# First attention of a decoder layer: row maxima taken by pairs of half-array products, values two steps behind

## What is computed

```python
q = (x @ Wq + bq).reshape(b, s, NH, HD).transpose(0, 2, 1, 3)
k = (x @ Wk + bk).reshape(b, s, NH, HD).transpose(0, 2, 1, 3)
v = (x @ Wv + bv).reshape(b, s, NH, HD).transpose(0, 2, 1, 3)
scores = jnp.einsum('bhqd,bhkd->bhqk', q, k) / jnp.sqrt(HD)
mod = jax.nn.sigmoid(x @ cg_W + cg_b + (cons_vec @ am_W + am_b))
scores = scores * mod.transpose(0, 2, 1)[..., None]
probs = jax.nn.softmax(scores, axis=-1)
ctx = jnp.einsum('bhqk,bhkd->bhqd', probs, v)
```

## Time and profile before

| | |
|---|---|
| median of 3 runs | 4114.03 us (4112.56 to 4117.21) |
| the profiled execution: time, span in the profile | 4116.67 us, 4114.9 us |
| granted TensorE clock, mean over the span | 0.905 of full speed |
| `attend_narrow`, first maximum to last copy | about 216 to 1074.5 us |
| its first score | 256.8 us |

### The profile page before, as it was taken

How to read it: one execution, slowest core, us unless ns; L and a number is a source line. 1 busy time by engine, 2 the same in 40 slices (tenths; PEclk the granted TensorE clock), 3 DMA queues, 4 the chain that set the end, 5 groups by cost and what they waited for, 6 DMA issues and landing times. The chain is left out here.

```text
span 4114.9 us, 58511 instructions
## 1 busy us (share of the span) xinstructions
PE 3605.2 (88%) x17196; PEld 2369.5 (58%) x17196; DVE 2374.9 (58%) x4296; ACT 1487.1 (36%) x2363; POOL 1038.5 (25%) x798
## 2 busy tenths in 40 slices
PE   8889999999799968799966587855899999999999
PEld 6644444545244426444445344434788888888888
DVE  5577777777266645566546588866433333333345
ACT  3236666666434333243433233321222222222222
POOL 4510000000033334333333400001333333333332
PEclk9979999999799988799987667767999999999999
DMA  7854444442333326533333665622000000000001
GB/s 248 275 66 63 63 63 63 63 63 37 80 83 82 82 72 216 151 83 82 85 114 128 136 84 81 90 76 74 16 15 15 0 15 15 15 0 15 0 5 36
DMA packets 218079, 303.68 MB, mean 74 GB/s; under 512 B 27679, under 2 KB 133511, under 8 KB 217927
## 3 DMA queue, kind: packets, MB, share of 16 engines
q1 hardware_dynamic: 213703, 297.65, 32.5%
q10 hardware_dynamic: 4224, 4.19, 0.3%
HBM read 182.23 MB, written 119.54 MB: 73 GB/s over the span
## 5 line engine op out<-in xcount | busy, mean ns | idle before, releaser
L564 DVE TENSOR_REDUCE an_m<-an_psm 128x1 f32<-128x1024 f32 x512 | 605.0, 1220 | 194.9 <-PE an_psm L488 193.3
L544 ACT ACTIVATE an_probs<-an_pst 128x512 f32<-128x512 f32 x1024 | 533.5, 603 | 258.4 <-PE an_pst L515 257.9
L2349 POOL TENSOR_TENSOR ex_hb<-ex_hid,ex_ha 128x512 fp32r<-128x512 f32 x288 | 375.7, 1305 | 773.8 <-DVE ex_ha L2430 773.8
L2400 ACT ACTIVATE ex_gated<-ex_pg 128x512 f32<-128x512 f32 x288 | 172.4, 598 | 926.1 <-PE ex_pg L47 926.1
L2428 DVE TENSOR_TENSOR ex_hid<-ex_gated,ex_pu 128x512 f32<-128x512 f32 x288 | 198.2, 688 | 480.6 <-PE ex_pu L47 478.1
L488 PE MATMUL an_psm<-an_ks,an_qs 95*128 95x512 f32 x1024 | 368.8, 444 | 33.4 <-DMA an_vs<-scr_v 29.8
L515 PE MATMUL an_pst<-an_qs,an_ks 96*128 96x512 f32 x1024 | 340.2, 411 | 10.8 <-issue 6.3
L488 PEld LDWEIGHTS an_psm<-an_ks,an_qs 95*128 95x128 f32 x1024 | 181.3, 199 | 270.8 <-issue 206.9
L2383 PE MATMUL ex_py<-ew_a,ex_hb 128*128 128x256 f32 x1152 | 321.7, 279 | 0.0
L2383 PE MATMUL ex_py<-ew_b,ex_ha 128*128 128x256 f32 x1152 | 321.6, 279 | 0.0
L2383 PE MATMUL ex_py<-ew_a,ex_ha 128*128 128x256 f32 x1152 | 321.4, 279 | 0.0
(11 more groups left out here) (358 smaller groups left out, 7057.9 us busy)
## 6 DMA issues: line engine op xcount, KB each, us to landing
an_qs<-scr_q SPq DMA_DIRECT2D x64, 256.0 KB, 11.6
an_ks<-scr_k SPq DMA_DIRECT2D x64, 256.0 KB, 13.5
ac_qs<-scr_xq SPq DMA_DIRECT2D x64, 256.0 KB, 7.7
ca_qs<-scr_cq SPq DMA_DIRECT2D x24, 512.0 KB, 8.3
ca_ks<-scr_ck SPq DMA_DIRECT2D x24, 512.0 KB, 10.0
mc_qs<-scr_mq SPq DMA_DIRECT2D x24, 512.0 KB, 8.7
mc_ks<-scr_mk SPq DMA_DIRECT2D x24, 512.0 KB, 10.3
scr_q<-in_ab SPq DMA_DIRECT2D x16, 512.0 KB, 2.8
```

The source lines that it names most:

```text
L544: act.activation(probs[:, s % 2, j], pst[:, (GH * s + j) % RING], ACT.Exp, scale=HD ** -0.5).then_inc(exp_done, 1)
L564: dve.tensor_reduce(m1[:, hq, col:col + 1], psm[:, n % 2], AX.XY, ALU.max).then_inc(mx_done, 1)
L2349: pool.tensor_tensor(hb[:, f], hid[:, f % 2], ha[:, f].bitcast(F32), ALU.subtract).then_inc(b_done, 1)
L2400: act.activation(gated[:, f % 2], pg[:, f % 2], ACT.Silu).then_inc(gated_done, 1)
```

## The change

It is in `attend_narrow` alone, but for ten semaphores of the row transfers, which `decoder_layer` now makes and passes in (`moved`).

- **Layout.** The low-by-low combination is dropped (three combinations, 48 rows). `qs` holds the 48 rows twice, at rows 0 to 47 and 64 to 111, with a row of maxima behind each copy. `ks` holds keys 0 to 511 in the upper half of the array's rows and keys 512 to 1023 in the lower half; where one half holds keys, the other holds zeros.
- **Maxima in pairs.** The two products of a unit now contract over 48 rows each, one in rows 0 to 47, one from row 64, into the two banks of `psm`.
- **Scores.** Still one product per head and step, now over all 128 rows, the other half's zero keys included.
- **Values two steps behind** (`LAG = 2`), with `probs` four steps deep, across the borders of groups too; after a score with j = 1, or at the end of the step for a first key block.
- **Units** run 14 steps ahead (`LEAD`), so the last four units of a group fall into its own first two steps.
- **The rows of maxima** go through POOL's queue: per row four writes, a wait, two reads (one per copy), a wait. SP keeps loads (13 a group instead of 9) and stores.
- **Smaller:** DVE negates inside the reduction (L569 goes) and no longer copies `pacc`; ACT copies both halves. POOL and DVE fill more blocks before the first group.

```diff
-        qs, ks = k.sb("qs", [LAST, NG, GH, S], FR), k.sb("ks", [LAST, NG, GH, S], FR)
+        qs, ks = k.sb("qs", [P, NG, GH, S], FR), k.sb("ks", [P, NG, GH, HALVES, S // HALVES], FR)
...
-        probs = k.sb("probs", [P, 2, GH, CH])
+        probs = k.sb("probs", [P, TURNS, GH, CH])
...
+                for r, (qp, kp) in enumerate(((0, 0), (0, 1), (1, 0))):
+                    if first and r == 2:
+
+                        sp.wait_ge(filled, QFILLS + FILLS * slot)
+                        sp.wait_ge(filled_first, KFILLS)
+                    for h in range(HALVES):
+                        at = slice(h * HROW + r * HD, h * HROW + (r + 1) * HD)
+                        sp.dma_start(qs[at, slot].bitcast(F32),
...
-                last = pe.matmul(psm[:, n % 2, kh], qs[0:MROW, slot, j, q0:q0 + P], ks[0:MROW, slot, j, kh * CH:(kh + 1) * CH],
-                                 start=True, stop=True)
-                if kh == 1:
-                    last.then_inc(mx_ready, 1)
+                for h in range(HALVES):
+                    at = slice(h * HROW, h * HROW + DATA)
+                    last = pe.matmul(psm[:, n % 2, h], qs[at, slot, j, q0:q0 + P], ks[at, slot, j, h], start=True, stop=True)
+                last.then_inc(mx_ready, 1)
+
+            def scores(G, slot, s, j):
+                qh, kc = divmod(s, KC)
+                h, c = divmod(kc, KC // HALVES)
+                n = GH * s + j
+
+                pe.wait_ge(exp_done, EXP0 + NST * G + last_use(n) + 1)
+                pe.matmul(pst[:, bank[n]], ks[:, slot, j, h, c * P:(c + 1) * P],
+                          qs[:, slot, j, qh * CH:(qh + 1) * CH], start=True, stop=True).then_inc(st_ready, 1)
...
+            def step(b, g, s, before, more):
...
+                ahead, n0 = units_of(s)
+                late = before is not None and before[2] % KC == 0
+                for j in range(GH):
+                    scores(G, g, s, j)
+                    if j == 1 and before is not None and not late:
+                        values(*before)
+                    if j % 2 == 0:
+                        if ahead == 0:
+                            unit(G, g, b, n0 + j // 2)
+                        elif more:
+                            unit(G + 1, (g + 1) % NG, b + (g + 1) // NG, n0 + j // 2)
+                if late:
+                    values(*before)
...
+                pool.wait_ge(m_ready, CPB * G + hq + 1)
+                pool.sem_inc(row_seen, 1)
                 turned = scr["m"][hq].rearrange("(c b r) -> b c r", b=4, r=32)
                 for q in range(4):
-                    sp.dma_start(turned[q], mrows[32 * q:32 * q + GH * NT, hq].bitcast(F32)).then_inc(m_out[hq], 16)
+                    pool.dma_start(turned[q], mrows[32 * q:32 * q + GH * NT, hq].bitcast(F32)).then_inc(m_out[hq], 16)
+                pool.wait_ge(m_out[hq], 64 * G + 64)
+                pool.sem_inc(row_seen, 1)
+                for h in range(HALVES):
+                    row = h * HROW + DATA
+                    pool.dma_start(qs[row:row + 1, slot, :, hq * CH:(hq + 1) * CH].bitcast(F32),
+                                   scr["m"][hq:hq + 1].rearrange("o (j n) -> o j n", j=GH)).then_inc(mrow_in[slot][hq], 16)
+
+                pool.wait_ge(mrow_in[slot][hq], 32 * uses + 32)
...
-                    dve.tensor_reduce(m1[:, hq, col:col + 1], psm[:, n % 2], AX.XY, ALU.max).then_inc(mx_done, 1)
+                dve.tensor_reduce(mneg[:, hq, col:col + 1], psm[:, n % 2], AX.XY, ALU.max, negate=True).then_inc(mx_done, 1)
...
-                dve.tensor_copy(ev[:, 1], pacc[:]).then_inc(acc_dve, 1)
```

More of the change, by code:

```diff
@@ L434, in store, with group @@
             def store(G, qh):
[L435 to L438, removed]
+                sp.wait_ge(acc_out, CPB * G + qh + 2)
                 sp.dma_start(scr["craw"][bass.ds(G * P, P), qh * CH:(qh + 1) * CH], ev[:, qh]).then_inc(ev_out[qh], 16)
-            def group(b, g, ahead):
+            def group(b, g, more, first):
                 G = b * NG + g
[L443 to L450, removed]
+                if more:
+                    load(G + 2, (g + 2) % NG, first)
+                for qh in range(CPB):
+                    store(G, qh)
@@ L452, in _ @@
             for qh in range(CPB):
                 sp.sem_inc(ev_out[qh], 16)
[L454 to L458, removed]
+            load(0, 0, True)
+            load(1, 1, True)
+            for g in range(NG):
+                group(0, g, True, g < 2)
+            with sp.Fori(1, B - 1) as b:
                 for g in range(NG):
-                    group(b, g, 2)
+                    group(b, g, True, False)
@@ new lines, in step, with rest, border @@
+                if late:
+                    values(*before)
+            def rest(b, g, more):
+                G = b * NG + g
+                for s in range(LAG, NSTEP):
+                    step(b, g, s, (G, g, s - LAG), more)
+            def border(b, g, more):
+                for s in range(LAG):
+                    step(b + (g + 1) // NG, (g + 1) % NG, s, (b * NG + g, g, NSTEP - LAG + s), more)
+            pe.sem_inc(pv_done, PV0)
+            pe.wait_ge(filled_first, KFILLS)
+            for n in range(PER * LEAD):
+                unit(0, 0, 0, n)
@@ L528, in _ @@
+            for s in range(LAG):
+                step(0, 0, s, None, True)
             with pe.Fori(0, B - 1) as b:
                 for g in range(NG):
-                    group(b, g, True)
+                    rest(b, g, True)
+                    border(b, g, True)
             for g in range(NG):
-                group(B - 1, g, g < NG - 1)
+                rest(B - 1, g, g < NG - 1)
+                if g < NG - 1:
+                    border(B - 1, g, g + 1 < NG - 1)
+            for s in range(NSTEP - LAG, NSTEP):
+                values(B * NG - 1, NG - 1, s)
@@ L534, in _ @@
         @block.scalar
         def _(act):
[L536 to L549, removed]
@@ new lines, in _ @@
+            act.sem_inc(exp_done, EXP0)
+            act.sem_inc(acc_out, 1)
+            for s in range(LAG):
+                step(0, s)
+            with act.Fori(0, B - 1) as b:
+                for g in range(NG):
+                    G = b * NG + g
+                    rest(G)
+                    border(G)
+                    copy_out(G, 1)
+            for g in range(NG):
+                G = (B - 1) * NG + g
+                rest(G)
+                if g < NG - 1:
+                    border(G)
+                copy_out(G, 1)
```

207 lines of the change are left out of this document (114 added, 93 removed).

## The result

The changed kernel takes 4281.59 us (median of 4 runs, 4278.49 to 4297.44) against 4115.62 for the kernel before (4 runs, 4112.56 to 4119.7): a ratio of 1.0419, interval 1.0402 to 1.0436. It is slower, as forecast, but by 166 us where 48 were predicted; the range ended at 4190. The profiled execution of after took 4279.64 us against 4116.67 before, +163.

The account below looks back on a forecast made before the run. PE was taken to bound the step. Units +75, values' wait -5, group borders -14, last group -5 and start -3 gave +48 on 4116.67, 4165; less 2.6 to the median, 4162 us. Range 3965 to 4190.

Parts of the forecast that it names:

- The step: PE, middle of a group: six changes of tile shape make a unit 0.86 us instead of 0.705, +75 us in all.
- Rivals 1 to 4: Steps: 1 free changes (0.24); 2 only way back costs (0.08); 3 second load uncovered (0.09); 4 halves serial, changes free (0.03).
- Groups: Units +75 us, values no longer waiting for ACT -5, group borders -14.
- The border's gain: Group borders: values spread over the next steps remove 0.94 us, 15 times, -14 us.
- Last group: Steps without maxima, values two steps behind: PE alone sets 2.14 us instead of 2.60, -5 us.
- Start: First score after 28 units instead of 32, with more loads: -3 us, 0 if the row is late by 3.
- The row of maxima: Row transfers on POOL's queue: 4.4 to 18 us each, with 18 to 20 us available, so nothing added.
- rival 5: A row of maxima over 20 us on POOL stalls PE by the excess; 5 us over would be 155; chance 0.02.
- the likeliest case: Every change of tile shape costs and weight loads overlap: 4140 to 4190 us, chance 0.50.

Follow-up runs that it names:

- the loads behind the row: Changed kernel, but SP issues the loads of the group after next only once the group's second row of maxima has landed: 4188.54 us, ratio 1.0172.
- maxima of 64 rows: Kernel before, with maxima contracting over the 64 rows that hold data instead of 95, no pairs: 4356.53 us, ratio 1.0456.
- scores in a half: Changed kernel with loads after the second row of maxima, and scores contracting over the 49 rows that hold their keys: 4087.36 us, ratio 0.9927.
- both units together: Changed kernel with loads after the second row of maxima, and both units of a step issued behind its first score: 4103.38 us, ratio 0.997.
- with the whole array: All of the change but its layout (96 rows, unpaired full-array products), with loads after the second row of maxima: 4114.0 us, ratio 0.9993.

## Why the prediction was wrong in size

Its time is the sum of terms, so each is held against its own measurement. The run with the loads behind the row isolates the row; it took 4184.70 us in its profiled execution, +68 on before, and after took another +95.

- **The step: right.** Forecast 3.39 us, measured 3.37; score to score across a unit 0.86 forecast, 0.86 measured; every change of tile shape pays, the two halves overlap. Rivals 1 to 4 asked for steps of 2.6, 2.97, 3.6 or a pair 0.235 apart, and none is there. The price of 0.195 a change (0.33 - 0.235 + 0.10), taken from the earlier trace rows, is confirmed from both sides:

| kernel | pairs | changes a step | step, us |
|---|---|---|---|
| before | no | 2 | 3.085 |
| maxima of 64 rows | no | 5 | 3.65 |
| scores in a half | yes | 2 | 2.60 to 2.62 |
| both units together | yes | 4 | 2.98 |
| after | yes | 6 | 3.37 |

Without pairs 0.565 / 3 = 0.188; with them (3.37 - 2.61) / 4 = 0.19. And 3.085 - 2.61 = 0.475 is what the pairs save, the forecast 0.47. The Trainium skill (TensorEngine Tiling (Array Packing), Key Properties) says that a change of tiling mode drains the TensorE. These steps agree, at 0.19 us a change, now for row tiles alone.

- **Groups: right.** +75 - 5 - 14 = +56 was forecast. Measured (54.10 - 50.30) x 15 = +57. The border's gain, too, is there in this kernel (54.10 against 16 x 3.37 = 53.92), but that is luck, there only because PE's longer step gives ACT its time: with the whole array, where PE's step is 3.07, it came to 0.94 - 0.83 = 0.11 a group instead of 0.94.
- **Last group: the sign was wrong, the size small.** Forecast -5, with steps of 2.14 us; measured 47.0 against 43.80, +3.2, with steps of 2.61 as before. PE's rows there:

```profile
1205.45 0.96 PE L536 MATMUL an_pst<-an_qs,an_ks 128*128 128x512 f32 x3
1206.64 0.98 PE L536 MATMUL an_pst<-an_qs,an_ks 128*128 128x512 f32 x2 [0.22 <-ACT an_probs L605]
```

The scores wait for ACT. The forecast had removed the values' wait for exp but not the scores' wait for a free bank of the ring of three: values of 1.00 us stand between two scores, and the ring lets PE run only three scores ahead of ACT. That reading is argued from these rows and was not tried with a longer ring.

- **Start.** -3 was forecast, "0 if the row is late by 3". With the loads behind the row the first score came at 251.5, -5.3; in the change it came at 262.8, +6.0, for the first row met the loads as well: POOL waited 13.81 us for its writes.
- **The row of maxima: the step that failed.** The prediction says of it "Nothing is added", and gave rival 5 a chance of 0.02 with "From 4.4 us on SP that is far". Rival 5 is what happened: 24 us, over both its 20 and the upper end of 18, though for 11 rows of the 31. The one number that it named as its sign of being wrong, score to score across a unit, came out as forecast, and the time was wrong all the same. Of the 95 us between the two profiled executions, 81.3 lie in groups 0 to 14 (915.2 us against 833.9 from the first score to the first of the last group), 11.3 in the start, and 2.3 behind the stage. The waits view from 300 to 1200 us (total, times, longest) puts 53.7 of the 81.3 to the waits themselves:

```profile
PE an_pst L536 <- DMA an_qs<-scr_m: 53.7, 11, 6.2
```

Another 33 lie in the steps behind them in the same eleven groups, at the lower clock, the first of 5.2 to 6.1 us instead of 3.37; groups 0, 4 and 8 lose 5 less than with the loads behind the row.

The error was to price the row by what it took in before, with the order that before had. The earlier trace rows is the row of the last group, where no load is in flight: the window gives a DMA share of 0.04 there, and 0.46 in a middle group. But a row from the middle would have said the same, for there SP's program order kept row and loads apart. SP's queue in before, in the middle of the stage:

```profile
568.08 1.70 SPq L426 DMA_DIRECT2D scr_m<-an_mrows  x4
570.82 0.58 SPq L428 DMA_DIRECT2D an_qs<-scr_m  x1
...
573.74 1.31 SPq L415 DMA_DIRECT2D an_qs<-scr_q  x1
...
593.54 1.99 SPq L426 DMA_DIRECT2D scr_m<-an_mrows  x4
598.37 0.60 SPq L428 DMA_DIRECT2D an_qs<-scr_m  x1
```

The row at 568.08 is 2.74 us from write to read, and the loads come only behind its waits, from 573.74. The other row of the group, at 593.54, meets their tail (DMA share 0.56 from 593.5 to 599.0) and takes 4.83. That was the hint in the trace of before, and the earlier trace rows leave it out, since they hold only the wait for the read. No row of before shows the writes at the start of the loads. The move to POOL was costed as a move of instructions between queues; it was also the removal of an order between two transfers.

The Trainium skill (DMA: Bandwidth & Descriptors, Issuing engines are not separate DMA queues) says that transfers issued by scalar, sync or gpsimd run on the same 16 DMA engines and interleave. The rows at 576 agree: POOL's writes held it for 8.73 us beside SP's loads, and for 1.65 without them.

- **What is left.** Sums of the stage: -5.3 + 60.0 + 3.2 = +57.9 for the run with the loads behind the row (the 60.0 has 3 us more than 57 at the first group and the loop's ends). The other 10 of its 68 lie behind the stage, where the code is the same: 3042.2 us from the stage's end in before, 3052.3 here, 3054.6 in after, 3047.8 in the run with units together. The ten profiled executions have 3042 to 3057, before the least, and the kernel before with 64-row maxima, one line of the stage away from it, has 3050.7. So it does not take the change to lengthen this part. What lengthens it stays open, and a difference of under some 15 us between the totals of two executions says nothing of the stage.

So the forecast of 4162 is 26 us off for the change that it thought it saw: with the loads behind the row the kernel takes 4188.54, just within the range of 4140 to 4190 that the likeliest case had for itself. The order that the diff dropped costs another 93.

## What to carry to other kernels

When a transfer moves to another queue, list what the old queue's program order kept apart, and price the transfer by a row that has the same traffic around it; if no row has it, the price is not known, and the chance of a late transfer is not 0.02. Packing products into parts of the array pays only where the changes of tile shape that it brings cost less than it saves: count them at about 0.19 us each first (0.47 us saved a step here, against four new changes at 0.76). A wait that vanishes because another engine became slower is not a gain to be kept: it comes back when that engine is fast again, as with the whole array here.

## What the runs showed of the hardware

- A change between tiles of few and of many rows costs 0.19 us at full clock (2.4 GHz), for 64 rows beside 96 in the kernel before, and for 48 beside 128. Scores of 96 beside maxima of 95 rows run as one stream, at 0.235 a product. What a change of columns costs by itself no run isolates.
- Two products in different halves of the array's rows start together even when one is a score and the other a maximum. In the run with scores in a half:

```profile
585.43 0.40 PE L538 MATMUL an_pst<-an_qs,an_ks 49*128 49x512 f32 x1
585.45 0.49 PE L528 MATMUL an_psm<-an_ks,an_qs 48*128 48x512 f32 x1
```

- Small transfers beside 13 large ones took 6.6 us (writes of 2 KB) and 12.6 us (reads of 8 KB) to land; with the loads behind the row POOL's wait for the same writes was 1.63 instead of 8.73.
- The granted clock followed the shape of the work and not only PE's idle time: 0.57 in a last group of 49-row scores that PE was busy with for 59.28 of 61.20 us, 1.00 with the same scores over 128 rows, busy 41.54 of 46.10. In the kernel before with 64-row maxima it stayed at 0.50 for 104.5 us behind a loop's end, in the one run of it that was profiled. In before the steps were back at 3.08 or 3.09 us with the third or fourth of that group. What makes it rise there is not settled by these runs.
